# A selective scan that reads y from its states in products over 32 rows, with C's columns kept in two copies

## The reference

```
dA = exp(dt * A)                                  # per head, state and token
h_t = dA_t * h_(t-1) + dt_t * B_t * x_t           # 8 states per head, 128 channels
y_t = sum over the states of h_t * C_t  (+ D * x_t)
y   = y back in the image's order, * silu(gate) + res, then out_proj and silu
x   = x + y;  then the experts: sum_e weight_e * (x_norm @ W_e + b_e)
```

## Time and profile before

| | |
|---|---|
| median of 3 runs | 1005.8 us (1005.25 to 1007.03) |
| the profiled execution | 1010.08 us, its span 1008.3 us |
| TensorE, products | 916.3 us busy, 91% of the span |
| TensorE, weight loads | 714.5 us, 71% |
| VectorE | 747.3 us, 74% |
| ScalarE | 534.5 us, 53% |
| GpSimd | 487.7 us, 48% |

### The profile page before, as it was taken

One profiled execution on the slowest core, in us unless ns is written; L12 is line 12 of the kernel. 1 busy time (PEld: TensorE's weight loads), 2 busy tenths in 40 slices (PEclk: granted clock), 3 DMA queues, 4 the chain that ended last, 5 costly groups with the idle time before them and its releaser, 6 DMA issues.

```text
span 1008.3 us, 15638 instructions
## 1 busy us (share of the span) xinstructions
PE 916.3 (91%) x4658; PEld 714.5 (71%) x4658; DVE 747.3 (74%) x2003; ACT 534.5 (53%) x1037; POOL 487.7 (48%) x549
## 2 busy tenths in 40 slices
PE   3999899999776787777799999999999999999997
PEld 3887788887454555445678777787777777787776
DVE  5677778564776778666778787788778787788875
ACT  2767677776987998776433332333333332333330
POOL 2145577887788788886544413344034431340000
PEclk8889899999788989778899999999999999999999
DMA  5227765547447444632531401413104131040001
GB/s 171 84 85 215 193 157 171 145 79 234 134 118 171 131 130 124 183 106 86 188 127 43 167 23 39 146 42 144 43 21 166 39 120 70 21 166 21 21 1 42
DMA packets 63690, 110.07 MB, mean 109 GB/s; under 512 B 18539, under 2 KB 44437, under 8 KB 60565
## 3 DMA queue, kind: packets, MB, share of 16 engines
q1 hardware_dynamic: 54388, 90.23, 28.6%
q0 software_dynamic: 7168, 18.03, 6.4%
q10 hardware_dynamic: 2080, 1.19, 0.5%
HBM read 61.51 MB, written 47.92 MB: 109 GB/s over the span
## 4 chain that ended last, share of the span: by engine, by line
PE 66%; DMA 10%; POOL 8%; DVE 6%; issue 4%; SPq 2%; ACT 2%; ACTq 0%; DVEq 0%; POOLq 0%
PE bank L1432 36%; PE bank L1166 8%; PE bank L1341 5%; PE bank L1368 5%; POOL sm L732 4%; DMA bc_scratch<-r 4%; DMA bl<-bc_scratch 3%; PE bank L1396 2%; SPq L460 2%; PE bank L1176 2%; PE bank L1194 2%; PE bank L1380 1%; DMA score_scratch<-score 1%; DVE kbd L1844 1%; DMA xin<-rows_scratch,turn 1%
## 5 line engine op out<-in xcount | busy, mean ns | idle before, releaser
L801 POOL TENSOR_TENSOR ssm<-ssm,rg 128x512 f32<-128x512 f32 x30 | 35.2, 1195 | 255.0 <-DVE ssm L1902 255.0
L1432 PE MATMUL bank<-wexph,xhl 128*128 128x512 f32 x512 | 144.1, 403 | 0.0
L1432 PE MATMUL bank<-wexph,cr 128*128 128x512 f32 x512 | 143.2, 401 | 0.0
L789 POOL DMA_INDIRECT xtm<-y_scratch,idxu x112 | 109.7, 980 | 61.3 <-issue 30.2
L732 POOL TENSOR_TENSOR sm<-sm,rg 128x512 f32<-128x512 f32 x96 | 122.7, 1278 | 29.9 <-DVE rg L1829 17.8
L1829 DVE TENSOR_TENSOR rg<-rg,bank 128x512 f32<-128x512 f32 x112 | 72.4, 679 | 50.5 <-PE bank L1294 43.6
L1432 PEld LDWEIGHTS bank<-wexph,xhl 128*128 128x128 f32 x512 | 93.3, 188 | 22.4 <-DVE xf L2008 1.7
L1432 PEld LDWEIGHTS bank<-wexph,cr 128*128 128x128 f32 x512 | 93.4, 189 | 21.8 <-DVE ysb L2008 1.7
L975 ACT ACTIVATE rg<-dists,aown 128x512 f32<-128x512 f32 x128 | 81.9, 722 | 0.0
L1432 PE MATMUL bank<-wexpl,xhl 128*128 128x512 f32 x256 | 80.7, 396 | 0.0
L1432 PE MATMUL bank<-wexpl,cr 128*128 128x512 f32 x256 | 80.4, 395 | 0.0
(11 more groups left out here) (309 smaller groups left out, 2092.1 us busy)
## 6 DMA issues: line engine op xcount, KB each, us to landing
xin<-in_x SPq DMA_DIRECT2D x16, 1024.0 KB, 5.4
res_gate_scratch<-rg SPq DMA_DIRECT2D x16, 1024.0 KB, 10.6
rg<-res_gate_scratch SPq DMA_DIRECT2D x8, 2048.0 KB
y_scratch<-ysb SPq DMA_DIRECT2D x16, 512.0 KB, 3.7
out<-stage SPq DMA_DIRECT2D x16, 512.0 KB, 2.7
rows_scratch<-stage SPq DMA_DIRECT2D x8, 580.0 KB, 7.2
bc_scratch<-r SPq DMA_DIRECT2D x16, 288.0 KB, 3.9
rows_scratch<-xr SPq DMA_DIRECT2D x6, 580.0 KB, 9.2
```

The source lines that it names most:

```text
L789: pool.indirect_dma_start(out=xtm[:, t, h * P:(h + 1) * P], out_offset=None, in_=y_d[b // GB].rearrange("q p s c -> (q p s) c"), in_offset ...
L1432: last = pe.matmul(bank[4 + i][:, :], x_[:, k, i * P:(i + 1) * P], w[:, 2 * ep * KC + k:2 * ep * KC + k + KC + 1:KC, :], start=(n + k == 0 ...
```

## The change

The states are no longer copied by tile. y_of multiplies the 32 rows of `hs` that hold a pair of tiles with 32 rows of C's columns, once for each tile of the pair. So that the product for one tile doesn't take in the other's states, the columns are kept in two copies: in `cwt` the rows of the odd tiles are zero, in `cwo` those of the even ones. Both come from the same bank in `columns`, by a copy with a scale of 0 or 1 per row (`odd`, made once with the constants). y_of(c, pair) now does half of both banks, where y_of(c, i) did one whole bank, so that both banks are complete only after its second call. TensorE waits for h_ready in place of hx_ready; `a_free` counts three; and in the last chunk both copies of y come after `gate_exp`.

```diff
--- before.py
+++ after.py
@@ -180,7 +180,8 @@
         bwx = sb("bwx", [P, 2 * (P + 16)])
         cw = sb("cw", [P, P])
         cwt = [sb(f"cwt{i}", [P, P]) for i in range(4)]
-        hx = [xf[:, i, :].rearrange("p (t c) -> p t c", c=P) for i in range(2)]
+        cwo = [[v[:, i * P:(i + 1) * P] for i in range(4)] for v in (ssm[:, 0, :], xf[:, 1, :])]
+        odd = sb("odd", [P, 2])
         dec = sb("dec", [P, 1])
         r6 = sb("r6", [S * ST, 6, P + SUB], F32R)
         bl = [sb(f"bl{i}", [P, S, P], F32R) for i in range(2)]
@@ -290,7 +291,7 @@
         s_full = signal("s_full", 1)
         s_free = signal("s_free", 1)
         a_full = signal("a_full", 2)
-        a_free = signal("a_free", 2)
+        a_free = signal("a_free", 3)
         b_full = signal("b_full", 1)
         dec_ready = signal("dec_ready", 1)
         args_ready = signal("args_ready", 1)
@@ -310,7 +311,7 @@
         st_full = signal("st_full", 1)
         dskip_ready = sem("dskip_ready")
         y2_full = [signal(f"y2_full{i}", 1) for i in range(2)]
-        hx_ready = signal("hx_ready", 1)
+        y_half = signal("y_half", 2)
         y2_used = [signal(f"y2_used{i}", 1) for i in range(2)]
         h_ready = signal("h_ready", 2)
         y_stored = [signal(f"y_stored{i}", 16) for i in range(2)]
@@ -396,6 +397,9 @@
         def dt_of(c):
             return xr[c.row][:, :, P]
 
+        def odd_columns(c):
+            return cwo[c.q > NT][c.four]
+
         def split3(hi_lo_w, hi_lo_x):
 
             return ((hi_lo_w[0], hi_lo_x[0]), (hi_lo_w[0], hi_lo_x[1]), (hi_lo_w[1], hi_lo_x[0]))
@@ -904,7 +908,9 @@
             def columns(c):
 
                 act.wait_ge(a_full.sem, a_full.at(c.q, 2))
-                act.activation(cwt[c.four][:, :], bank[A_BANK][:, 0:P], ACT.Copy).then_inc(a_free.sem, 1)
+                for i, v in enumerate((cwt[c.four][:, :], odd_columns(c))):
+                    act.activation(v, bank[A_BANK][:, 0:P], ACT.Copy, scale=odd[:, i:i + 1]).then_inc(
+                        a_free.sem, 1)
 
             def store_rows(b):
 
@@ -989,16 +995,6 @@
                 act.activation(ysb[c.two][:, h * GB:(h + 1) * GB, :].rearrange("p t c -> p (t c)"),
                                bank[SY_BANK + h][:, :], ACT.Copy).then_inc(y2_used[h].sem, 1)
 
-            def states_by_tile(c):
-
-                act.wait_ge(h_ready.sem, h_ready.at(c.q, 2))
-                if c.q > 1:
-                    for h in range(HEADS):
-                        act.wait_ge(y2_full[h].sem, y2_full[h].at(c.q - 2, 1))
-                for t in range(ST):
-                    last = act.activation(hx[c.two][:, t, :], hs[c.four][:, :], ACT.Copy, scale=own_rows[:, t:t + 1])
-                last.then_inc(hx_ready.sem, 1)
-
             def body(q):
                 c = Chunk(q)
                 decays(c, 0, 2)
@@ -1007,7 +1003,6 @@
                     block_decays(Chunk(q + 1))
                 if q:
                     decays(c, 2, S)
-                    states_by_tile(c)
                     for h in range(HEADS):
                         y_rows(Chunk(q - 1), h)
                 else:
@@ -1063,22 +1057,20 @@
                 rows_high(last)
                 block_decays(last)
                 decays(c, 2, S)
-                states_by_tile(c)
                 for h in range(HEADS):
                     y_rows(Chunk(CHUNKS - 3), h)
                 z_high(0)
                 columns(last)
                 decays(last, 0, S)
                 silu_t(0, FRONT_BANKS)
-                states_by_tile(last)
                 for h in range(HEADS):
                     y_rows(c, h)
                 copy_t(0, 0, FRONT_BANKS)
                 deviation3(0)
                 x3_high(0, 0, FRONT_BANKS)
-                y_rows(last, 0)
                 gate_exp(0, 0)
-                y_rows(last, 1)
+                for h in range(HEADS):
+                    y_rows(last, h)
 
             last_chunks()
 
@@ -1294,18 +1286,23 @@
                     pe.matmul(bank[BC_BANK + s % 3][:, :], bl[c.two][:, s, :], cr[c.two][:, s, :], start=True,
                               stop=True).then_inc(bc_full[s % 3].sem, 1)
 
-            def y_of(c, i):
-
-                pe.wait_ge(hx_ready.sem, hx_ready.at(c.q, 1))
+            def y_of(c, pair):
+
+                pe.wait_ge(h_ready.sem, h_ready.at(c.q, 1))
                 pe.wait_ge(k_ready.sem, k_ready.at(c.q, 2))
-                pe.wait_ge(y2_used[i].sem, y2_used[i].at(c.q, 0))
-                dst = bank[SY_BANK + i]
-                pe.matmul(dst[:, :], cwt[c.four][:, :], hx[c.two][:, GB * i:GB * (i + 1), :].rearrange("p t c -> p (t c)"),
-                          start=True, stop=False, skip_group_check=True)
-                for b in range(GB):
-                    last = pe.matmul(dst[:, b * P:(b + 1) * P], kbd[:, GB * i + b, :], xr[c.row][:, GB * i + b, 0:P],
-                                     start=False, stop=(b == GB - 1), skip_group_check=True)
-                last.then_inc(y2_full[i].sem, 1)
+                for i in range(HEADS):
+                    dst, rows = bank[SY_BANK + i], slice(PART * (2 * i + pair), PART * (2 * i + pair + 1))
+                    if pair == 0:
+                        pe.wait_ge(y2_used[i].sem, y2_used[i].at(c.q, 0))
+                    else:
+                        pe.wait_ge(y_half.sem, y_half.at(c.q, i + 1))
+                    for b, own in ((2 * pair, cwt[c.four]), (2 * pair + 1, odd_columns(c))):
+                        pe.matmul(dst[:, b * P:(b + 1) * P], own[rows, :], hs[c.four][rows, :],
+                                  start=(b == 0), stop=False, skip_group_check=True)
+                    for b in (2 * pair, 2 * pair + 1):
+                        last = pe.matmul(dst[:, b * P:(b + 1) * P], kbd[:, GB * i + b, :], xr[c.row][:, GB * i + b, 0:P],
+                                         start=False, stop=(b == GB - 1), skip_group_check=True)
+                    last.then_inc((y2_full[i] if pair else y_half).sem, 1)
 
             def body(q):
                 c = Chunk(q)
@@ -1560,6 +1557,8 @@
                         dskip_ready, 1)
                 own.did(dve.tensor_reduce(own_rows[:, :], ident[:, :].rearrange("p (t x) -> p t x", x=2 * S), AX.X,
                                           ALU.add))
+                own.settle()
+                own.did(dve.tensor_reduce(odd[:, :], own_rows[:, :].rearrange("p (g e) -> p e g", e=2), AX.X, ALU.add))
                 for i in range(2):
                     r = slice(SUB * i, SUB * i + SUB)
                     own.did(dve.tensor_copy(tri[r, :], cumu[r, r]))
```

## The result

The changed kernel takes 1032.6 us (median of 4 runs, 1025.94 to 1035.41) against 1005.5 us for the kernel before on the same chip (4 runs): a ratio of 1.028, 95% interval 1.0233 to 1.0318. The prediction was 1008.9, range 1004.3 to 1014.0. The sign was right, the size was wrong by a factor of nine. Now and then an execution of any of these kernels, of the one before too (one of 1039.8 us at a mean clock of 0.818), shows a lower granted clock than the others and takes longer; the ratios leave such executions out.

The account below looks back on a forecast made before the run. The prediction took three rings of waits to bound the scan, not ScalarE's masked copies. Slow chunks +3.5, start -0.1, end +1.7 and clock recovery -2.0 gave +3.1 us on 1005.8: 1008.9 us, range 1004.3 to 1014.0.

Parts of the forecast that it names:

- Coming back: Scan chunks starting at the low clock: shorter TensorE idle stretches turn two in five fast, -2.0 us.
- three rings: Scan: r6's store and loads, 12.8 us; GpSimd's adds, 14.5 us; y_of, ScalarE's copies and next decay, nearly as long.
- TensorE's part: In y_of: alternating 32-row and 128-row products costs 0.5 us a call, bounds 0 and 0.9.
- ScalarE's column copies: Ahead of the next chunk's first decay: two scaled copies for one cost about 0.4 us, bounds 0.1 and 0.5.
- The start: Chunks 0 and 1: one more copy +0.4 us, ScalarE less late in chunk 1 gives back 0.5; net -0.1.
- The end: Chunk 15 and output projection: decay wait +0.4, chunk 14's y_of +0.3, chunk 15's two calls +1.0; together +1.7 us.
- GpSimd's stretch: From chunk 10 until about 449 us, bound by GpSimd's adds: over 2 us of cover, so no loss.
- The rivals: Whole kernel: free alternation, 1006.7 us, chance 0.23; faster clock and fewer collisions, 1002.6, 0.13; weight loads not overlapped, 1014.6, 0.14.
- Much slower: In y_of: weight loads of 32-row products can't overlap the product before; +8.8 us, 1014.6 us, chance 0.14.

Follow-up runs that it names:

- rows64: Changed kernel with each product from the states over 64 rows instead of 32, order untouched; 1014.2 us.
- filler: Changed kernel with step products 1 and 5 of each chunk issued twice, over all 128 rows; 1018.6 us.
- full_filler: Changed kernel with its state products over all 128 rows and five of the eight step products of a chunk issued twice; 1004.3 us.
- full_rows: Changed kernel with its products from the states over all 128 rows instead of 32, same count, columns and order; 1003.0 us.
- halves_side: Kernel before with four masked copies instead of eight and two 64-row, 512-column products, both issued in the first y call; 1003.7 us.
- b_32rows: Kernel before with its 512-column product from the states cut to 32 rows, masked copies and order kept; 1013.4 us.
- Two_columns: Kernel before with C's columns copied twice, with a scale from a tile, masked copies kept; 1003.2 us.
- split: Kernel before with the 512-column product from the states issued as four of 128 columns, all 128 rows; 1002.2 us.
- same_rows: Changed kernel with a call's four state products first, all over the same 32 rows, then the four within-chunk products; 1009.4 us.
- grouped: Changed kernel with a call's four 32-row products first, alternating between two row groups, then the four within-chunk products; 1004.9 us.
- once: Changed kernel with all eight state products of a chunk in the first y call, in two groups of four; 1012.6 us.
- filler_32b: Changed kernel with an extra copy of step products 1 and 5 of each chunk, cut to 32 rows; 1068.4 us.
- after: The changed kernel itself, against the kernel before; 1032.6 us, ratio 1.0233 to 1.0318.

## Why the prediction was wrong, step by step

**The clock, which is the step that failed.** The prediction's "Coming back" said that TensorE's shorter idle stretches would turn two in five slow chunks fast, -2.0 us. I took an idle stretch as the only thing that lowers the clock and took for granted that a chunk which starts at the lower level comes back within its first half, as the slow starts of before did. Both fail with products over few rows. The clock fell with no idle stretch over 0.95 us in the 6.5 us before (286.9 us), and chunks 3, 5 and 11 never came back. The slow starts didn't get fewer either: among chunks 1 to 9 there were five again, 1, 3, 4, 5 and 6. The term of -2.0 measured about +25: the five chunks above, the dearer calls in them included. rows64 (same durations in a call, more rows, 15 us less), filler (more full-row work, 12 us less) and full_filler (about the same load, all rows, nothing lost) show that it is the products over few rows and not the load: about half of the loss goes with the rows alone (rows64), and whether the changes of shape have a share in the rest isn't separated. The Trainium skill, TensorE: Matmul & The Clock Gate, Part 1, ties the level to how busy TensorE has been and warns of idle gaps only; chunk 5, at the lower level with TensorE busy for 17.91 us out of 17.91, disagrees.

**What bounds the kernel.** That ScalarE's copies weren't worth their time was right, and full_rows and halves_side bear it out. That three rings bound the scan was right for before. The list lacked the one ring that the change made: TensorE's own work in a chunk, about 10.4 us at the upper level and about 18 at the lower. In before that can't be seen, because no chunk stays at the lower level. It could have been worked out from chunk 2 of before, with the columns of the earlier trace rows:

```profile
284.60:297.10 12.50, 11.56 (x56) 7.55 (x56) 9.65 (x24) 10.29 (x32) 10.29 (x14) 0.75 0.46 129
```

TensorE is busy for 11.56 us at a mean clock of 0.75, which makes an estimate of 11.56 x 0.75 / 0.50 = 17.3 us at the lower level, longer than any ring named; b_32rows measured 17.0.

**TensorE's part.** Priced at 0.5 us a call with bounds of 0 and 0.9; measured 0.61 (2.39 - 1.78). That held. But it was laid only on chunks 2, 5 and 7 (+3.5). Chunks 2 and 5 lost 3.8 and 5.4 us, for the other reason: chunk 2 started at the upper level and fell in its middle, chunk 5 stayed at the lower. Chunk 7 ran at the upper level throughout and still took 14.45 us in place of 12.83, for which no run gives a cause. Which chunks start low changes from run to run, so naming them was false precision.

**ScalarE's column copies.** The two copies come 0.25 us apart and last 0.35 (329.16), so the size, 0.4 us, was about right (the 0.29 us that it is worked out from stands in no row; 2.45 / 8 is 0.31). They were to show up as VectorE waiting for the decay; at chunk 5's start it waits 2.97 us for product 0 (332.48), and from 255 to 520 us it waited for the decay ten times, never over 1.0 us (8.2 us in all; in before four times, 6.6 us, from 255 to 500). TensorE, which the prediction took to be covered, waited for the second copy too: seven times, 4.2 us in all, against 0.2 us for the one copy of before. But it does so in full_rows as well, with the same 4.2 us, and that kernel loses nothing that can be told. Two_columns puts the whole at 0 to 4.4 us, full_rows at up to 2.6.

**The start** (-0.1): chunks 0 and 1 took 27.0 us in place of 29.3, but with 12.7 and 12.9 us in full_rows and 14.3 and 13.0 in split they vary by as much between executions; so this isn't settled.

**The end** (+1.7) was 4.2 us, 2.6 up to the gate products and 1.6 behind. The mechanism was as named, the calls on the chain, but at the lower level, which chunk 14's fall had handed on (the first call of chunk 14 took 4.67 us, 488.37 to 493.04, in place of 3.56 in before, 468.47 to 472.03, the end of which the earlier trace rows shows).

**GpSimd's stretch** (nothing): wrong. Chunk 11 lies in it and lost 3.6 us; the cover of over 2 us that I claimed didn't hold at the lower level. Chunk 14, which comes behind that stretch and ahead of the end, stood in no term of the sum and lost 6.9.

**The rivals.** None held it. "Much slower" had the right half of a mechanism, that small products behind one another in the same rows don't overlap; same_rows puts that at 0.45 us for four, and that kernel lost 9 us in all. Its 1014.6 us was the top of my imagination for a reason: every case was summed at the clock levels of before, or at higher ones.

## What to carry to other kernels

Where TensorE alternates between its two clock levels, work out each loop body once more wholly at the lower level; if that is longer than the ring that bounds the loop now, anything that keeps the clock down costs the difference in each pass, and the loop can stay there for many passes. In this kernel products over a fraction of the rows did that, even where they took little time. What helped was to put a call's products over different row groups next to each other (grouped, halves_side) or to keep all rows in use (full_rows); putting all of a chunk's into one call (once) helped less. And an engine whose work is on no ring gives nothing back when it is relieved, however busy it is.

## What the runs showed of the hardware that I had not expected

- The granted clock fell from 1.00 to 0.50 while TensorE was at work, with idle stretches of at most 0.95 us in the 6.5 us before (chunk 2, 286.9 us), and stayed at 0.50 over 123.8 us in which TensorE was busy for 120.8 (filler_32b).
- Two kernels with the same durations call by call differ by 1.4% of the time, with 32 and with 64 rows in use (after, rows64). Added full-row products made a kernel faster by 1.2% (filler).
- A change of shape costs about 0.2 us at the upper level: 0.64 in place of 0.43 to 0.45 us for each group of the alternation, in all but the last of a call. It is the same with 64 and with 32 rows.
- Products over different row groups into different banks run side by side even when they are issued group by group: four in 0.64 us against 1.09 us over the same rows; two of 512 columns in 1.11 us against 1.05 for one.
